# A graph network layer with nucleus attention: guessed starting points for the threshold searches, a reordered tail of the first step, two earlier loads

## What is computed

```python
def _top_p_attention(X, W1, W2, W3):
    q = X @ W1.T @ W2.T
    k = X @ W3.T
    probs = softmax(q @ k.T, axis=-1)                  # 4096 x 4096
    idx = argsort(-probs); sp = take_along_axis(probs, idx); cs = cumsum(sp)
    keep_sorted = cs - sp < 0.9                        # top-p, scattered back to mask
    A = probs * mask
    return A / maximum(A.sum(-1, keepdims=True), 1e-12)
...
R = S + eye(N); R = R / R.sum(-1, keepdims=True)
for n in range(2):
    A = _top_p_attention(Xa, W1, W2, W3)
    Xf = R @ Xf;  Xa = A @ Xa
    Z = Z + Xf @ U1[n].T + Xa @ U2[n].T
h = layernorm(X + Z) * ln_g + ln_b
out = layernorm(x + h)
```

## Time and profile before

| | us |
|---|---|
| median of 3 runs | 1705.38 (1704.26 to 1706.78) |
| the profiled execution's own time | 1707.06 |
| its span | 1704.9 |

### The profile page before, as it was taken

How to read it: one execution, slowest core, us unless ns; L and a number is a source line. 1 busy time by engine, 2 the same in 40 slices (tenths; PEclk the granted TensorE clock), 3 DMA queues, 4 the chain that set the end, 5 groups by cost and what they waited for, 6 DMA issues and landing times. The chain is left out here.

```text
span 1704.9 us, 18073 instructions
## 1 busy us (share of the span) xinstructions
PE 1536.4 (90%) x4753; PEld 886.7 (52%) x4753; DVE 1319.2 (77%) x3739; ACT 813.6 (48%) x1301; POOL 235.6 (14%) x272
## 2 busy tenths in 40 slices
PE   7999999877999999998999999995267988988996
PEld 4555556434555555554555656653134544544553
DVE  6788888656677777776899999998968788796554
ACT  4555555312555555564444444443122836734444
POOL 2010210212000000001011111122210211311322
PEclk9999999988999999999999999997578999998998
DMA  7466666462455555555566666670000000000000
GB/s 260 173 152 151 182 190 181 109 236 96 163 187 187 188 197 203 203 203 201 184 167 171 162 195 195 196 175 1 2 3 1 1 7 7 8 1 8 7 7 13
DMA packets 53084, 211.92 MB, mean 124 GB/s; under 512 B 22096, under 2 KB 30864, under 8 KB 32512
## 3 DMA queue, kind: packets, MB, share of 16 engines
q1 hardware_dynamic: 49728, 210.59, 39.6%
q0 software_dynamic: 3264, 0.30, 0.2%
HBM read 206.63 MB, written 4.48 MB: 124 GB/s over the span
## 5 line engine op out<-in xcount | busy, mean ns | idle before, releaser
L1272 ACT ACTIVATE psL<-psL,umax 128x1024 f32<-128x1024 f32 x256 | 278.5, 1088 | 296.2 <-DVE umax L1755 288.3
L1761 DVE MAX8 cand<-psL 128x8 f32<-128x256 f32 (+1 forms) x640 | 371.9, 583 | 56.9 <-PE psL L904 46.9
L903 PE MATMUL psL<-kA,mq 128*128 128x512 f32 x512 | 297.5, 581 | 3.0 <-ACT psL L1272 1.6
L873 PE MATMUL psO<-adj_in,xf 128*128 128x512 f32 x512 | 241.6, 596 | 4.9 <-POOL adj_in L608 4.9
L873 PE MATMUL psO<-adj_in,xn 128*128 128x512 f32 x512 | 242.5, 597 | 3.6 <-DMA adj_in<-in_adjT 1.9
L1084 PE MATMUL psO<-ebuf,xn 128*128 128x512 f32 x512 | 241.7, 593 | 0.0
L2028 DVE SCALAR_TENSOR_TENSOR ebuf<-ebuf 128x1024 f32<-128x1024 f32 x128 | 156.7, 1225 | 99.1 <-PE psO L1084 92.6
L904 PE MATMUL psL<-kB,mq 66*128 66x512 f32 x512 | 202.5, 395 | 0.0
L1450 ACT ACTIVATE ebuf<-psL 128x1024 f32<-128x1024 f32 x128 | 129.6, 1019 | 150.6 <-PE psL L1126 109.6
L1382 ACT ACTIVATE ebuf<-psL 128x1024 f32<-128x1024 f32 x128 | 131.0, 1023 | 134.2 <-PE psL L1053 134.2
L1138 PE MATMUL psO<-xf,xa 128*128 128x512 f32 x340 | 167.0, 615 | 12.4 <-DVE xf L2257 9.4
(11 more groups left out here) (366 smaller groups left out, 2051.8 us busy)
## 6 DMA issues: line engine op xcount, KB each, us to landing
adj_in<-in_adjT SPq DMA_DIRECT2D x128, 1024.0 KB
adj_in<-in_adj SPq DMA_DIRECT2D x32, 2048.0 KB, 7.7
xaT<-in_xT SPq DMA_DIRECT2D x4, 512.0 KB, 5.3
xa_dram<-xa SPq DMA_DIRECT2D x8, 256.0 KB, 7.9
out<-t SPq DMA_DIRECT2D x8, 256.0 KB
list_dram<-ids,place POOLq DMA_INDIRECT x64
rel_prob<-cut_dram SPq DMA_DIRECT2D x32, 2.0 KB
cut_dram<-ncut SPq DMA_DIRECT2D x16, 2.0 KB
```

The lines of the kernel that those rows point to most:

```text
L873: last = nc.tensor.matmul(psO[:], fs[:, j, :], adj_in[:, r % RING, j % JQ, :], start=(j == 0), stop=(j == JT - 1))
L903: nc.tensor.matmul(o, qA[:, t * P:(t + 1) * P], kA[:, c:c + BI], start=True, stop=False)
L1272: nc.scalar.activation(ps[:], ps[:], ACT.Exp, bias=umax[:, bass.ds(i * UB + k, 1)], scale=1.0, accum_out=usum[:, bass.ds(i * UB + k, 1)]). ...
L1761: last = v.max(cand[:, t % 2, at + c * 8:at + c * 8 + 8], psL[(turn + k) % 3][:, c * WIDE:(c + 1) * WIDE])
```

## The change

- **Start of the search.** `guess` replaces the first halvings. From the mass of the sorted elements of a row (for a hard row the stored norm is now the reciprocal of that mass; it is gathered by one more indirect DMA per tile into `hmass`/`hmasses`) and the row's total it works out a first try.
- **Step 0:** the guess is the only try: the four halvings, the chord and its pass are gone; the pass `below`, the chunk maxima, 5 sorting rounds and the threshold follow at once.
- **Step 1:** two passes (4 half passes), each followed by `narrow`, which moves the try between the two nearest sums; then as before, with 48 sorted elements (6 rounds) in place of 40. There are 12 search steps in place of 19; ACT's 32 pieces, `summed` and `chord` are gone. FIRST_PAIR, WITHIN and ONE_AHEAD place the new steps.
- **The chunks** of the remainder interleave finer (32 runs of 8 elements in place of 8 runs of 32).
- **The flag** is also set where the last try lies under the target.
- **Tail of step 0:** two more quarters are loaded ahead (EARLY_LOADS = 2), and PE's 8 products on them move ahead of the tile's logits. Block 7's first 16 products stay ahead of the flag, its last 16 stand behind the first `mix_q` of the mixing. `prepare_q(c + 1)` moves behind the flag. POOL's `add_self(7)` moves behind the loop.
- **Ranking:** the placing part is 9 DVE instructions per block in place of 10. `hard` rows get norm 1/kept.

```diff
-    FIRST = 4
-    NEXT = 40
-    BIAS = 10.0
+    NEXTS = [40] + [48] * (STEPS - 1)
+    AHEAD_OF = [(25.0,)] + [(10.0, 10.0, 22.0)] * (STEPS - 1)
...
-                    held = FLOWS * PARTS + RING
+                    held = FLOWS * PARTS + RING + EARLY_LOADS
...
+                        nc.gpsimd.indirect_dma_start(
+                            out=hmass[:], out_offset=None, in_=norm_dram[s],
+                            in_offset=bass.IndirectOffsetOnAxis(ap=gid[:, 1:2], axis=0),
+                            bounds_check=N - 1, oob_is_err=False).then_inc(g["h_mass"], 16)
...
-                    for j in range(RING * JQ // 2, RING * JQ):
+                    for j in range(RING * JQ // 2, (RING + EARLY_LOADS) * JQ):
                         adj_part(FLOWS, j)
...
-                    for j in range(RING * JQ, JT):
+                    for j in range((RING + EARLY_LOADS) * JQ, JT):
                         adj_part(FLOWS, j)
-                    for a in range(FLOWS, NB):
-                        pe.wait_ge(g["r_o_sb"], a + 1)
-                        to_rows(a)
-                        if a + 1 < NB:
-                            for j in range(JT):
-                                adj_part(a + 1, j)
-                    pe.wait_ge(g["r_n_sb"], NB)
+                    pe.wait_ge(g["r_o_sb"], NB - 1)
+                    to_rows(NB - 2)
+                    for j in range(JT // 2):
+                        adj_part(NB - 1, j)
+                    pe.wait_ge(g["r_n_sb"], NB - 1)
                     with pe.Fori(0, tiles) as c:
-                        prepare_q(c + 1)
                         pe.wait_ge(g["h_flag"], c + 1)
                         nc.tensor.matmul(psS[:, 0:1], ones[:], hflag[:], start=True, stop=True).then_inc(g["h_flags"], 1)
                         pe.wait_ge(g["h_mid"], c + 1)
                         pe.wait_ge(g["h_exp"], c * NU + NU)
+                        prepare_q(c + 1)
                         prepare_logits(c + 1)
...
                     mix_q(0)
+                    for j in range(JT // 2, JT):
+                        adj_part(NB - 1, j)
+                    pe.wait_ge(g["m_q_lo"], 1)
+                    to_rows(NB - 1)
                     mix_block(0, None, True)
...
+            def guess(st, sums, top_, mass, ref, number):
+                link(v.tensor_reduce(ttotal[:, here], sums, AX.X, ALU.add))
+                v.tensor_scalar(ttarget[:, here], ttotal[:, here], TOP_P, None, ALU.mult)
...
+                link(v.reciprocal(hin[:], mass))
+                link(v.scalar_tensor_tensor(out=hout[:], in0=ttotal[:, here], scalar=hin[:], in1=tupper[:, here],
+                                            op0=ALU.subtract, op1=ALU.add))
...
+            def narrow(st, e):
+                link(v.scalar_tensor_tensor(out=haim[:], in0=hpart[:, 0:1], scalar=hpart[:, 1:2], in1=tinv[:, here],
+                                            op0=ALU.add, op1=ALU.mult))
...
-                        for k in range(1, FIRST + 1):
-                            halve(weights, rest, k)
-                        chord()
-                        above(weights, rest)
-                        settle_chord()
+                        guess(0, hsum[:, bass.ds(turn, 1), :].rearrange("p o u -> p (o u)"), htop_out[:], hmass_out[:], href_out[:], gid_out[:, 0:1])
                         below(weights, rest)
...
+                        if n < 4:
+                            part_sum(c, n % 2, ALU.is_lt)
+                            if n % 2 == 1:
+                                narrow(tile_slot(c), n // 2)
+                        if n in (4, 6):
+                            part_sum(c, (n - 4) // 2, ALU.is_lt)
+                        if n in (5, 7):
+                            part_largest((n - 5) // 2)
...
-                    FIRST_PAIR = {k: k for k in range(18)}
-                    FIRST_PAIR[19] = 18
-                    WITHIN = {0: 5, 1: 6, 3: 7, 4: 8, 5: 9, 6: 10, 9: 11, 10: 12, 12: 13, 14: 14, 16: 15, 17: 16, 18: 17, 19: 18}
-                    BEGIN_AT, SUMMED_AT, FOURTH_AT = 14, (21, 30), 31
+                    FIRST_PAIR = {0: 0, 2: 1, 4: 2, 6: 3, 8: 4, 9: 5, 11: 6, 12: 7, 14: 8, 16: 9, 18: 10, 19: 11}
+                    ONE_AHEAD = {22: 0, 27: 1}
+                    WITHIN = {0: 2, 2: 3, 5: 4, 6: 5, 8: 6, 10: 7, 13: 8, 15: 9, 17: 10, 19: 11}
+                    BEGIN_AT = 14
```

372 lines of the change are left out of this document (147 added, 225 removed).

## The result

The changed kernel takes 1669.01 us (median of 4 runs, 1666.41 to 1669.76) beside 1705.95 us for the kernel before: a ratio of 0.9782 with a 95% interval of 0.9765 to 0.9799. The direction was right; the gain, 36.9 us, is 54% of the predicted 68.3, and the time lies 6 us above the range. The profiled execution took 1669.76 us, its span is 1668.0, so the span shrank by 36.9 us.

The account below looks back on a forecast made before the run. It took DVE's chain to bound step 1's first search, DVE and PE step 0's, and waits at the flags the mixing. Terms 12.8 + 12.5 + 15 + 12 + 14 + 1 + 1 = 68.3 gave 1637 us, range 1618 to 1663.

Parts of the forecast that it names:

- Small instructions: DVE's searches: 0.20 us if waited for, 0.07 if not; guess 3.3 us, first narrow 2.7, second 3.0.
- rival (4): Small DVE instructions cost 0.20 us each, waited for or not: 11 us less gain, 1648 us; chance 0.05.
- tile 0: Search of step 1's first tile, up to the mixing: 12.5 us gained, bounds 7 and 13.
- Step 0: Search and tail of step 0: its mixing begins 11.0 us earlier, plus 1.7 from the clock; 12.8 us, bounds 6 and 16.
- Ranking: Ranking stage of step 1, bound by DVE: one small instruction less per block gains 1 us.
- Second halves: Step 1's mixing, the intervals behind the pairs' flags: steps at 22 and 27 replace the summing, 1 us gained.
- Pair 0 and pair 1: Step 1's mixing up to each pair's flag: 15 us gained (bounds 10 and 26) and 12 us (bounds 7 and 20).
- Rival (1): The mixing gives less, PE waiting for DVE at new places: 20 us instead of 41, 1658 us; chance 0.16.
- Pair 2: Step 1's mixing, third pair to its flag: 14 us gained, 3.3 of it from the clock; bounds 8 and 19.3.
- (3): Slower: the guess misses in a tile and DVE takes a bisection of 120 us, 1757 us; chance 0.10.
- (2): The mixing gives more: pairs come half way to PE's floors, 65 us instead of 41, 1620 us; chance 0.09.
- (5): The tails gain nothing, since round trips over POOL and SP end last there: 1662 us; chance 0.04.

Follow-up runs that it names:

- q and flag edits: Two edits of the changed kernel: low half of the next tile's q after mask 8, not 9 (alone 1662.1 us); flag's product one unit later (alone 1664.7 us).
- fastest kernel: Changed kernel with q and flag edits, maxima after mask 7, second step of tile two ahead after mask 30, two thrown-away products: 1649.2 us.

## Why the prediction was wrong

- **What bounds the kernel, and where.** Right in the main. The chains of DVE in both first searches, the flags, and the placement of waits in the mixing are where the time is.
- **Small instructions.** Right in kind: those not waited for start 0.07 us after the one ahead (365.48, 365.56, 365.62), so rival (4) is out. The Trainium skill ("VectorE: DVE Perf Modes", section "The DRAIN you can't avoid") says that chaining without semaphores skips nothing, and also that a next instruction that is not held starts earlier; these rows fit the second sentence. The size was off in step 1: the beginning takes 4.07 us (3.3 predicted, 3.42 in step 0), the two `narrow` 3.25 and 3.8 (2.7 and 3.0). Instructions with two scalar operands or two columns take 0.21 to 0.29 us; and two one-element instructions, one beside GpSimd's last scatter and one beside its addition, take 0.76 and 0.55 us where the same ones take 0.16 and 0.22 elsewhere, which is 0.9 us of the excess. The three together are 2.1 of the 2.8 us that **tile 0** gave less (9.7 instead of 12.5); the low half of q for tile 1 is late by the same 2.1, and its logits take 7.0 us at the half clock instead of 5.9.
- **Step 0**, 12.8 predicted, 11.4 measured at the end of its mixing. Maxima at no extra cost, PE and DVE ending together, and a full clock for the first mixing units (2.0 us, 1.7 predicted): right. The step that failed here is "the first gather needs the stores only some 14 us later": the list's scatter has to land before the gather's first load, and the gather waits 4.8 us longer for it behind the two loads (7.36 instead of 2.57 us; runs with 0 and 1 load). I had named the loads' lateness as the risk, not their effect on the list.
- **Left out of the sum:** the step from one stage to the next. The clock fell at the start of step 1's ranking and took 3.9 us. I counted the clock only where it gave something back. With the gaps filled it stayed up (three kernels of three); part of the 3.9 us may be the luck of the profiled execution. The Trainium skill ("TensorE: Matmul & The Clock Gate", section "HAM oscillation — how this bites in real kernels") tells of gaps that throw the array back; this trace has a fall behind gaps of 0.8, 1.3 and 0.7 us, at 0.63 us a product instead of 0.40, but the same gaps are followed by the full clock in the kernel before and in two of the runs.
- **Ranking**, 1 predicted, 0.35 measured.
- **Second halves.** This step failed worst, and it is the main step that failed: "steps at 22 and 27, beside 2.8 us of PE per unit with some units of lead: 1 us" was 10.3 us in the other direction. I counted DVE's work against PE's units (39.9 of 50 us, it fits) and did not line up what else stands at mask 27: ACT's centring ahead of it, the next block's q and cut rows behind it, GpSimd's three instructions beside it. The runs with the step at masks 25 and 30 and with less work on GpSimd show it; the step at mask 30 gives back 9.9 us of the two intervals, though only 5.4 of the whole mixing, since a part of the loss moves on to the pairs behind.
- **Pair 0 and pair 1**, 15 and 12 predicted, 11.2 and 5.6 measured. Rival (1) named the mechanism, PE waiting for DVE at `z_add` and then `hq`, and I gave it 0.16; these waits were there before (9.45 and 7.07 us) and shrank less than I took. The sum of DVE's work was too good as well: its busy time falls by 5.2 us in pair 1 (53.1 to 47.9), where I had a net of 7.8, and of the waits for ScalarE's exponential, of which I took 4 us for pair 1, there were only 3.2 in that interval. In other profiles of the same mixing pair 1 reaches its flag in 58.6 to 58.9 us, a gain of 9; its second half is longer there, so the sum of the mixing is the same. The mask, the half pass and the mask in front of the low half of q are 7.05 and 3.42 us of wait: the new search steps put half passes of 2.4 us at masks 8 of both pairs. The q and flag edits give most of these terms back: pair 0 takes 75.5 and 75.2 us to its flag with the one or the other and 71.4 with both, pair 1 55.7 with both and the step at mask 30.
- **Pair 2**, 14 predicted, 13.5 measured: with no tile two ahead, the reckoning by DVE's removed and added work holds, and so does the clock's part: from flag to `mix_last` it is 5.6 us (8.8 in the earlier trace rows).
- **The rivals.** (3) is out: no bisection in any tile. (1) was nearest: its 20 us in place of 41 is what the whole mixing gave (434.1 to 414.1), but as 30.3 us in the three intervals to the flags less 10.3 in the second halves. Its 1658 is 11 us too low for what lies outside the mixing: the clock (3.9), tile 0 (2.8), step 0 (1.4), and smaller terms. (2) and (5) are out. (2)'s price did not add up: the bounds of the three pairs are 65.3 us, which gives 1613, and half way to them 53, which gives 1625, not 1620. In the same way the terms half way to their bounds give about 1623 to 1651 and not 1620 to 1655; by neither correction would 1669 have come into the range.

In the order of the sum (step 0, clock, ranking, tile 0, pair 0, second halves, pair 1, pair 2): 11.4 - 3.9 + 0.4 + 9.7 + 11.2 - 10.3 + 5.6 + 13.5, and -0.6 behind the last `mix_last`, is 37.0 against 68.3. Of the missing 31, the edits give back about 20. What remains in the fastest kernel, some 12 us, can be read off its profile: 2.8 us at the start of step 0's mixing (412.1 instead of 409.3, where profiles of one code differ by 4.6), 2.8 in tile 0 of step 1, and 6.8 in the mixing, whose five intervals of the table are 71.4, 49.5, 57.0, 49.1 and 48.8 us. In each of the first two pairs VectorE also reads the flag into a register, which takes 3.85 us in which it does nothing else (1419.58 to 1423.43 in the changed kernel). In pair 1 it took 3.97 us before the change too, but in pair 0 1.65 before and 3.91 after, and in pair 2 1.60 and 1.61. What makes it long or short is not shown, and no run took that read away, so its share of pair 0's shortfall and of the 6.8 us stays open.

## What to carry to other kernels

When work is cut into steps between the units of a pipeline, removing half of a step's work says little; write down for each unit what else is queued on that engine ahead of and behind the step, who delivers to it, and how many units of lead the consumer has. Move a step first to a unit where nothing else stands, and only then count the sum. A bulk load sent out early is free only if no small transfer that the path waits for goes out beside or behind it; and a short gap between stages can cost the clock in one profile and not in the next, so compare several profiles before you explain a few microseconds by it.

## What the runs showed of the hardware

- **VectorE beside GpSimd.** A half pass takes 2.35 us, and 3.36 beside GpSimd's instructions on 128x512 elements; a one-element instruction 1.11 us instead of 0.22; with the step moved to mask 30, the cut rows' instructions, now beside GpSimd, take 0.81 and 1.64 us instead of 0.42 and 0.74. Those of them with two inputs in SBUF fit the Trainium skill, "SBUF — State Buffer", section "Who interferes with whom": such an instruction and a GpSimd instruction that reads SBUF block one another. The cast of 0.81 us has one input; there the same section has a mode of casts that contends as well.

```profile
1333.25 0.81 DVE L2171 CAST cuth<-rel_prob 2x512 fp32r<-2x512 f32 x1
1333.85 1.33 POOL L784 TENSOR_TENSOR t<-t,xn 128x512 f32<-128x512 f32 x1
1334.10 1.64 DVE L2172 SCALAR_TENSOR_TENSOR mq<-cuth,sign,cum_keep 2x512 fp32r<-2x512 f32 x1
```

- **Small scatters behind bulk loads.** Behind four indirect scatters of 128 rows GpSimd waits 2.57 us for them to land when no extra load of 1 MB goes out on SyncE's queue ahead of them, 3.57 with one (10 us ahead of the first scatter), and 7.36 with two (8.3 and 2.7 us ahead).
- **The clock.** Three gaps of 0.8, 1.3 and 0.7 us after full work were followed by the half level in seven profiled kernels, by the full one in one and by something between in two, although the ten run the same instructions up to there. In six of the seven the product behind the second gap was already slow (1.07 to 1.12 us instead of 0.66). What decides it is not shown.
